# Graph attention on one core: edge counts taken per 25 destinations, in batches of 8 blocks with 250 columns, instead of per 50 in batches of 15 with 500

## The reference, cut to what matters

```python
x, src, dst                      # 1250 nodes x 768; 40000 edges, sorted by dst
h  = gat_conv(layernorm(x), edges + self loops, W1, ..., heads=4)     # attention over incoming edges
e  = leaky_relu(alpha_src[src] + alpha_dst[dst], 0.2)
e  = exp(e - segment_max(e, dst)[dst]); alpha = e / segment_sum(e, dst)[dst]
out = segment_sum(xl[src] * alpha, dst)
h  = relu(layer_norm(h)) + (x @ Wr1 + br1); then a second gat_conv with one head, layer_norm, residual
x  = x + h;  x = x + moe(layernorm(x))                                # 8 experts, 2 taken per row
```

## Time and profile before

| | us |
|---|---|
| three timed runs | 1230.8, 1230.85, 1231.26 (median 1230.85) |
| the profiled execution, its own time | 1235.26 |
| its span in the trace | 1233.5 |
| busy in the span: PE, DVE, ACT, POOL | 1140.9, 708.3, 363.6, 143.9 |
| mean granted TensorE clock | 0.97 of full speed |

### The profile page before, as it was taken

One profiled execution on the slowest core, in us unless ns is written; L12 is line 12 of the kernel. 1 busy time (PEld: TensorE's weight loads), 2 busy tenths in 40 slices (PEclk: granted clock), 3 DMA queues, 4 the chain that ended last, 5 costly groups with the idle time before them and its releaser, 6 DMA issues.

```text
span 1233.5 us, 14852 instructions
## 1 busy us (share of the span) xinstructions
PE 1140.9 (92%) x4512; PEld 726.2 (59%) x4513; DVE 708.3 (57%) x1597; ACT 363.6 (29%) x632; POOL 143.9 (12%) x281
## 2 busy tenths in 40 slices
PE   6798899999999999998999998999997398989994
PEld 3354456665547888875565555656664255656662
DVE  4799987519714776796764614686776222323322
ACT  1121111133235777751010014531000132323331
POOL 3000000000000000001000100002222112323232
PEclk9899999999999999999999999999998599999998
DMA  9543432261112510106221200193434546463423
GB/s 238 187 156 121 165 130 104 104 224 34 50 50 80 183 43 1 34 23 180 74 68 42 67 25 25 44 307 97 123 115 139 175 149 223 141 223 128 137 79 101
DMA packets 52952, 141.59 MB, mean 115 GB/s; under 512 B 8633, under 2 KB 16985, under 8 KB 52641
## 3 DMA queue, kind: packets, MB, share of 16 engines
q1 hardware_dynamic: 40673, 107.39, 26.8%
q0 software_dynamic: 8480, 23.16, 6.0%
q10 hardware_dynamic: 3744, 10.35, 2.8%
HBM read 82.89 MB, written 62.27 MB: 118 GB/s over the span
## 4 chain that ended last, share of the span: by engine, by line
PE 46%; issue 34%; DVE 10%; DMA 7%; DVEq 1%; POOL 1%; ACT 1%; SPq 0%; ACTq 0%; POOLq 0%
PE PSA L1605 11%; PE PSA L1555 9%; PE PSA L1544 7%; PE PSA L1678 7%; PE PSA L1690 6%; DVE RW2X L765 3%; DVE RW2X L767 2%; DMA RX<-in_x 2%; DMA RW<-out,RW 1%; PE PSA L1667 1%; DVE RB L776 1%; PE PSA L1388 1%; DMA out<-RW 1%; PE PSA L1362 1%; DMA RW<-xs_d 1%
## 5 line engine op out<-in xcount | busy, mean ns | idle before, releaser
L1528 PE MATMUL PSA<-RW2X 125*125 125x257 f32 x800 | 174.0, 380 | 0.7 <-ACT RB L1167 0.7
L1528 PEld LDWEIGHTS PSA<-RW2X 125*125 125x125 f32 x800 | 149.7, 188 | 25.4 <-ACT RB L1167 1.5
L1605 PE MATMUL PSA<-RW2X,RW 125*125 125x385 f32 (+1 forms) x360 | 122.4, 489 | 0.0
L826 DVE TENSOR_TENSOR RW2X<-RW2X 125x625 f32<-125x625 f32 x80 | 64.9, 811 | 87.7 <-ACT RW2X L1202 87.5
L765 DVE TENSOR_SCALAR RW2X<-RW2X 125x500 bf16<-125x500 int16 x375 | 99.6, 346 | 25.3 <-PE PSA L1388 14.3
L1678 PE MATMUL PSA<-RW2X,RW 128*128 (+1 forms) x300 | 107.0, 509 | 5.9 <-ACT RW L1293 5.9
L1362 PE MATMUL PSA<-RW,RX 128*125 128x512 f32 x240 | 110.5, 611 | 0.9 <-ACT RX L1110 0.9
L1555 PE MATMUL PSA<-RW2X,RX 128*125 128x384 f32 x320 | 109.4, 498 | 1.0 <-DVE RW2X L910 1.0
L1544 PE MATMUL PSA<-RW2X,RX 128*125 128x384 f32 x320 | 105.1, 487 | 2.2 <-ACT RX L1213 1.4
L1459 PE MATMUL PSA<-RW,RX 128*125 128x512 f32 x240 | 105.6, 594 | 0.0
L1388 PE MATMUL PSA<-RW2X 125*125 125x500 bf16 x375 | 87.7, 387 | 16.3 <-DVE RW2X L767 16.3
(11 more groups left out here) (271 smaller groups left out, 1307.6 us busy)
## 6 DMA issues: line engine op xcount, KB each, us to landing
xs_d<-RB SPq DMA_DIRECT2D x10, 3108.0 KB, 12.1
RW2X<-in_L_ffn_W SPq DMA_DIRECT2D x16, 1152.0 KB, 8.7
RW<-xs_d ACTq DMA_DIRECT2D x26, 388.5 KB
res_d<-RB SPq DMA_DIRECT2D x10, 448.0 KB
RX<-res_d SPq DMA_DIRECT2D x10, 448.0 KB
RX<-in_x SPq DMA_DIRECT2D x12, 336.0 KB
RX<-adm_d SPq DMA_DIRECT2D x6, 610.4 KB
xr_d<-RW2X SPq DMA_DIRECT2D x10, 336.0 KB
```

The lines of the kernel that those rows point to most:

```text
L826: v.tensor_tensor(e[:, 0], e[:, 0], e[:, 1], ALU.max).then_inc(exp_joined, 1)
L1528: last = mm(ps[n % 7][0:TP, 0:XW], ering[:, (p * NT + m) % EBUF, 0, i * TP:(i + 1) * TP], xl[:, m, p // 2, :], start=(m == 0), stop=(m == ...
L1605: last = mm(ps[PAIR[t % 3][c]][0:TP, 0:DW - c], p2[m][:, t * TP:(t + 1) * TP], xl2[:, m, c, 0:DW - c], start=(m == 0), stop=(m == NT - 1))
```

## The change

- A range has 25 destinations, there are 50 ranges, a batch has 8 blocks. `ohk` has 250 columns a block: comparisons of 125x250, matmuls of 250 columns.
- There are five pairs of buffers (`OB` = 5), each half as large or less; the table has 50 words and its running sums are taken by five.
- Where one range stood, a pair of ranges stands now. On DVE, `window(2 * w)` and `window(2 * w + 1)` follow each other. On PE, one `hist(w)` clears a bank of 500 columns, then reads the word and runs the loop for each of the two ranges, and adds the self loops for both. The columns of the two ranges alternate in the bank: the output of a matmul is 10 runs of 25 fp32, 50 apart. ACT copies as before.
- Scratch areas (`iscr`, `gbc`, `gi`, `win_in`) move to make room.

```diff
-GC = 15
-WD, NW = 50, 25
+GC = 8
+WD, NW = 25, 50
+OB = 5
+PW, NP = 2 * WD, NW // 2
...
-        ohk_w = a(GC * NT * WD, TP)
-        ohk = ohk_w.bitcast(BF16).rearrange("p (s c q) -> p s c q", s=2, c=GC)
+        ohk = a(OB * GC * NT * WD // 2, TP).bitcast(BF16).rearrange("p (s c q) -> p s c q", s=OB, c=GC)
...
-                b = w % 2
+                b = w % OB
...
-                    window(w)
+                    window(2 * w)
+                    window(2 * w + 1)
                     if w == 2:
...
-                hp = ps[2 + b][0:TP, 0:NT * WD]
-                mm(hp, zb[:, 0:TP], zb, start=True, stop=False, skip_group_check=True)
-                with pe.Fori(0, trips) as r:
-                    pe.wait_ge(onehot_ready[b], pe.snap(off + r + 1))
-                    for c in range(GC):
-                        last = mm(hp, ohq[:, b, c * TP:(c + 1) * TP], ohk[:, b, c, :], start=False, stop=False,
-                                  skip_group_check=True)
-                    last.then_inc(onehot_free[b], 1)
...
+                bank = ps[2 + w % 2][0:TP, 0:NT * PW]
+                mm(bank, zb[:, 0:TP], zb, start=True, stop=False, skip_group_check=True)
+                for i in range(2):
+                    n = 2 * w + i
+                    b = n % OB
+                    word = pe.value_load(tab_i[0:1, n:n + 1], min_val=512, max_val=(1 << 24) - 1)
...
+                    hp = r3(bank, NT)[:, :, i * WD:(i + 1) * WD]
+                    with pe.Fori(0, trips) as r:
+                        pe.wait_ge(onehot_ready[b], pe.snap(off + r + 1))
+                        for c in range(GC):
+                            last = mm(hp, ohq[:, b, c * TP:(c + 1) * TP], r3(ohk[:, b, c, :], NT), start=False,
+                                      stop=False, skip_group_check=True)
+                        last.then_inc(onehot_free[b], 1)
```

More of the change, by code:

```diff
@@ L313, in gnn_ffn @@
         small_kept = sem("small_kept")
-        onehot_ready = [sem(f"onehot_ready{i}") for i in range(2)]
-        onehot_free = [sem(f"onehot_free{i}") for i in range(2)]
+        onehot_ready = [sem(f"onehot_ready{i}") for i in range(OB)]
+        onehot_free = [sem(f"onehot_free{i}") for i in range(OB)]
         hist_done = sem("hist_done")
@@ L739, in _ @@
             dve.wait_ge(range_rows, 1)
[L740 to L744, removed]
+            own.link(v.tensor_copy(tab_f[:, 0:2, :], ps[2][0:1, 0:128].rearrange("p (a b) -> p a b", a=2)[:, :, 0:NW]))
+            turns = [tab_f[:, i, :].rearrange("p (a b) -> p b a", b=OB) for i in range(4)]
+            for b in range(OB):
+                last = v.tensor_tensor_scan(turns[2][:, b, :], ones[0:1, 0:NW // OB], turns[1][:, b, :], 0.0, ALU.mult, ALU.add)
             own.link(last)
             own.link(v.tensor_tensor(tab_f[:, 2, :], tab_f[:, 2, :], tab_f[:, 1, :], ALU.subtract))
-            own.link(v.scalar_tensor_tensor(tab_f[:, 3, :], tab_f[:, 2, :], 32.0, tab_f[:, 1, :], ALU.mult, ALU.add))
+            own.link(v.scalar_tensor_tensor(tab_f[:, 3, :], tab_f[:, 2, :], 64.0, tab_f[:, 1, :], ALU.mult, ALU.add))
             own.link(v.scalar_tensor_tensor(tab_f[:, 3, :], tab_f[:, 3, :], 512.0, tab_f[:, 0, :], ALU.mult, ALU.add))
@@ L1117, in hist_keep @@
                 act.wait_ge(hist_done, w + 1)
[L1118 removed]
+                s.copy(cnt[:, :, w * PW:(w + 1) * PW], r3(ps[2 + w % 2][0:TP, 0:NT * PW], NT)).then_inc(hist_kept, 1)
             def small_keep(t):
@@ L1385, in hist @@
-                with pe.Fori(0, trips) as r:
-                    pe.wait_ge(onehot_ready[b], pe.snap(off + r + 1))
-                    for c in range(GC):
-                        last = mm(hp, ohq[:, b, c * TP:(c + 1) * TP], ohk[:, b, c, :], start=False, stop=False,
-                                  skip_group_check=True)
-                    last.then_inc(onehot_free[b], 1)
-                d0 = w * WD
-                for t in range(d0 // TP, (d0 + WD - 1) // TP + 1):
-                    n0, n1 = max(d0, t * TP), min(d0 + WD, (t + 1) * TP)
-                    last = mm(ps[2 + b][0:TP, t * WD + n0 - d0:t * WD + n1 - d0], identb, identb[:, n0 - t * TP:n1 - t * TP],
+                bank = ps[2 + w % 2][0:TP, 0:NT * PW]
@@ L1395, in hist @@
+                d0 = w * PW
+                for t in range(d0 // TP, (d0 + PW - 1) // TP + 1):
+                    n0, n1 = max(d0, t * TP), min(d0 + PW, (t + 1) * TP)
+                    last = mm(ps[2 + w % 2][0:TP, t * PW + n0 - d0:t * PW + n1 - d0], identb, identb[:, n0 - t * TP:n1 - t * TP],
                               start=False, stop=True, skip_group_check=True)
                 last.then_inc(hist_done, 1)
-            for b in range(2):
+            for b in range(OB):
                 pe.sem_inc(onehot_free[b], 1)
```

32 lines of the change are left out of this document (15 added, 17 removed).

## The result

| | before | after |
|---|---|---|
| median of the timed runs, us | 1230.8 (1228.4 to 1231.3) | 1215.4 (1212.2 to 1217.5) |
| the profiled execution, its own time and its span | 1235.26, 1233.5 | 1212.22, 1210.5 |
| mean granted clock in it | 0.97 | 0.964 |

The ratio is 0.9865 with a 95% interval of 0.9842 to 0.9887: **16.6 us less, between 14 and 19.4**; the two medians of the table differ by 15.4. A second set of runs of the same kernel gave 0.9872 (0.9846 to 0.9897). 1208 was forecast, 23 us less.

The account below looks back on a forecast made before the run. DVE was taken to pace ranges 0 to 14 and PE ranges 15 to 24; gains of 8.7, 2.4 and 14.5 us less 2.5 made 23.1, so 1230.85 became 1208 us, own range 1203 to 1213, with rivals 1198 to 1224.

Parts of the forecast that it names:

- Steps 1 and 5: DVE, first half: ranges of pair 14 ready 8.7 us earlier, less 0.8 for uncovered gaps in its stream (bounds 0 and 2).
- Step 2: PE at pair 14: ends 0.87 us behind the last data instead of 3.23, so 2.4 us less.
- Step 3: PE, pairs 15 to 24: ten pairs at 1.45 us less each, 14.5 us in all.
- Step 4: PE at the hand-over between the halves: one loss to a lowered clock after longer idling, 1.7 us off the gain.
- waits behind the second read of the word in the second half: PE, second half: sign that would show the prediction wrong; the second read was costed at nothing.
- PE waits for DVE in every pair up to 14: PE, first half: expected sign, with no waits from pair 15 on; waits about 27 us in all instead of 16.
- DVE keeps ahead there: Pairs 15 to 24: a tile of three takes PE 21.4 us and DVE 19.3, so PE paces.
- The price per comparison (0.13 or 0.26): DVE, 250 columns: two rivals to 0.195 us; 0.13 gives 1199 us, chance 0.08; 0.26 gives 1225, chance 0.06.
- the bank at 0.212: PE matmuls: rival that 250 columns in runs of 25 cost what 500 do; 1224 us, chance 0.08.
- The fast mode: DVE comparisons: rival that 250 columns lose it, 0.39 us each; 1270 us, slower than before, chance 0.05.
- two batches: Ranges touching 9 blocks: rival that a few second batches make the gain vanish; counted as no change, chance 0.03.
- The rival of the clock: PE: clock stays low past the hand-over, 3 to 8 us more lost; 1211 to 1216 us, chance 0.12.

Follow-up runs that it names:

- contiguous: The changed kernel with a pair's two ranges one behind the other in the bank, 250 columns in one run; 1215.0 us, ratio 0.9881.
- filler: The changed kernel plus PE matmuls of zeros into an unused bank ahead of word reads in tiles 1 to 5; 1212.6 us, ratio 0.9847.
- again: The changed kernel unchanged, run and traced once more; 1215.9 us, ratio 0.9872 to the kernel before.
- two_filled: The changed kernel with two pairs of buffers instead of five, and PE matmuls of zeros ahead of each tile's third-pair word reads; 1228.9 us, ratio 0.9982.

## Why the prediction was right, and where it was off

The direction, the sign of every large term and the place of the gain were right; the time came out 7 us above the forecast and within its range. By the steps of the sum, each counted from the arrival of x in the two profiled executions:

| step | forecast | measured |
|---|---|---|
| 1 and 5, DVE has the data of pair 14 earlier | 8.7 - 0.8 = 7.9 | 5.8 |
| 2, PE ends pair 14 behind it | 2.4 | 2.3 |
| 4, the clock at the hand-over | -1.7 | 0 |
| 3, the ten pairs of the tail | 14.5 | 11.8 |
| sum | 23.1 | 19.9 |

**Steps 1 and 5.** The last data of pair 14 and the comparisons that follow it, DVE's timeline of after:

```profile
153.21 1.19 DVE L767 TENSOR_TENSOR RW2X<-RW2X 125x1000 bf16<-125x1000 bf16 x1
154.31 1.65 DVE L765 TENSOR_SCALAR RW2X<-RW2X 125x250 bf16<-125x250 int16 x8
```

The next comparisons start 154.31 - 33.12 = 121.2 us behind x; before it was 162.57 - 35.57 = 127.0. The prices were right: 0.195, 1.11, 5.34 a pair. The first pair came 8.9 us behind x instead of 9.3, some 0.5 for a forecast 0.6. Off was the size of the gaps: I bounded them by 2 us, took 0.8, and they cost 2.8. Four of them stand between the two ranges of a pair, 0.47 to 0.51 us each and 2.0 together: in the third pair of the tiles 3, 4 and 5 and in the second of tile 2. At each of the four places DVE's sequencer reads the second word in about 0.9 us (878 to 906 ns, at 59.3, 91.5, 116.4 and 140.4). The other 0.8 is spread over smaller gaps. The second of the four:

```profile
91.77 1.19 DVE L767 TENSOR_TENSOR RW2X<-RW2X 125x1000 bf16<-125x1000 bf16 x1
93.36 1.65 DVE L765 TENSOR_SCALAR RW2X<-RW2X 125x250 bf16<-125x250 int16 x8 [0.40 <-issue]
```

I had priced exactly this, "one of 0.9 ... would cost 0.5 us here", and then left the long read where it was, once a tile, by counting on reads behind another range to be short. That is the part of the prediction that failed: the places where such a read can fall had doubled, and with 15 comparisons in front of it 1.1 + 14 x 0.13 + 0.6 = 3.5 us had stood against 5.91 of the engine, where it is 2.6 against 2.67 now.

**Step 2** held. PE's self loops of pair 14 start at 155.42, 1.1 us behind the start of those comparisons, where before it was 165.94 - 162.57 = 3.4. (The forecast counted both from PE's first matmul on the last data, which gives the same difference.)

**Step 3** was mis-sized twice. The three interrupted pairs take 3 x 0.6 = 1.8 us. The prediction put the second read "at nothing where PE is behind", on the ground that the sequencer runs ahead by whole groups of matmuls. Behind 12 matmuls of 512 columns no pair of the tail is interrupted; behind 12 of 8 columns the long reads come through. The other 0.8 is 160 matmuls at 0.113 instead of 0.108, and 0.7 of it is what the runs of 25 cost by the run contiguous. The sign that would be wrong, "waits behind the second read of the word in the second half", did appear.

**Step 4** was a loss that did not count. The stage lost 11.9 us of clock instead of 5.1, in four dips instead of two, but all before the hand-over, where PE only came to its next wait later; the runs with filler show it. "PE waits for DVE in every pair up to 14" was wrong as well: it waits 13 times in seven of these pairs, and last at 145.04, in pair 13. Its waits came to 20.6 us and not to about 27: the 6.8 us more that it lost to the clock there are about the difference.

**What had no term.** The sum takes from the five pairs of buffers that "DVE keeps ahead there", and prices nothing for them. Two pairs bring the time back to 1235 us. So the change's smaller ranges are worth nothing without the depth, and the rival that I left out, the tail at half clock behind waits for a late DVE, was the most expensive mechanism in the traces: some 15.6 us by the clock and 6 by the waits. No run has the depth alone, five pairs with the ranges of before. The trace of before speaks against a gain from it: in the first half DVE never waits for a buffer, as its waits of 36 to 162 us show (the other one there is for x), and in the second PE is busy throughout at full clock.

```profile
DVE RW2X L765 <- issue: 11.0, 15, 1.6
```

**The rivals.** The price per comparison (0.13 or 0.26) and the bank at 0.212 are excluded by their rows, 0.195 and 0.113. The fast mode was not lost. No range took two batches, as the page's group of L765 counts 400 comparisons, 50 x 8:

```profile
L765 DVE TENSOR_SCALAR RW2X<-RW2X 125x250 bf16<-125x250 int16 x400 | 82.8, 282 | 18.6 <-issue 18.1
```

The Trainium skill's formula (VectorE: DVE Perf Modes, TRN2 errata) would have given 0.126 for the 250 columns; the trace has 0.195. The rival of the clock had 1211 to 1216, and the measured time lies there, but not by its mechanism: the last dip of the stage ends at 149.4, before pair 14, and the clock is 1.00 from 155.40 to 229.70.

**The last 3 to 4 us.** The stage is 19 to 20 us shorter, the timed runs put it at 15 to 16.6. The intervals reach up to 19.4, and the table of traces shows two things outside the stage that move by 5 and 10 us from one execution to the next. The clock points at the second of them. The clock lost over a whole span (span x (1 - mean granted clock)) is 47.1 us on average in the six executions of again and 34.5 in the eleven of before that were timed beside them, 12.6 more; the traces place 13.7 - 5.1 = 8.6 of this in the stage, where it costs nothing, and the 4 that are left would be behind it. This is an estimate: only one of the six was traced. Why the clock should be lower there after the change is not shown. The trace in which 23.0 us of span went, as forecast, agreed by chance: 2.5 of them were x and 0.8 the rest.

## What to carry to other kernels

When a producer and a consumer take turns being the bound, the depth of buffers between them is a term of its own, and it should be priced in the half where the consumer is the bound: a late producer there costs its waits, and in the traces here the clock behind them cost more than twice as much. A loss of clock counts only where the engine is the bound; look who sets the pace before adding it. And when a step is made shorter, every fixed cost that was hidden behind it (a register read of 0.3 to 0.9 us) has to be counted again in each place where it now stands, against the margin that is left.

## What the runs showed of the hardware

- A comparison on DVE with a per-partition number from SBUF takes 0.26 us at 500 columns and 0.195 at 250, so halving the columns took a quarter off; in a straight line through the two, 0.13 us stay at no columns.
- Matmuls of 250 bf16 columns stand 0.109 us apart into one run of PSUM, 0.113 into ten runs of 25.
- The read of a word into a register takes 0.3 or 0.9 us, for the same instruction, in one trace (a few between them, 0.4 to 0.7). What makes one long is not shown.
- Behind waits of 0.64 and 2.05 us PE's matmuls ran at the lower level of the clock (L1363: 8.18 instead of 5.39 us for twelve), and in the one trace with matmuls of zeros in the place of the waits they did not.
- Executions of one kernel differ in time as they differ in clock. two_filled went from 0.977 to 0.964 and over 17 us of time in twelve executions; with the lost clock, span x (1 - mean granted clock), taken off they lie within 4 us. The kernel before spread by up to 14 us in 17 executions and the other changed ones by 4 to 11.
